# One packed word a record, and scatters without staging copies, in a graph network kernel

## The chip, the cores and the metric

The kernel runs on one NeuronCore of a Trainium2 chip. The metric is the time of one execution on the device in microseconds (us), median of several executions. The engines are TensorE (PE), VectorE (DVE), ScalarE (ACT), GpSimd (POOL) and SyncE (SP); 16 DMA engines move data between the on-chip memory (SBUF) and device memory. Indirect transfers, which take one row address a partition from a column of SBUF, are issued by POOL; plain ones by SP.

## The reference

6250 nodes with 128 features, 100000 edges with a source and a destination. Two GATv2 attention layers with three heads (self loops added), with batch norms and a skip path, and then one attention layer with eight heads, which sums over the edges of each source:

```python
edge_index = jnp.stack([src, dst])
h = jnp.maximum(_layernorm(x), 0.0)
x = x + _L0_gnn_ref(h, edge_index, ...)      # two GATv2 layers: softmax over the edges of each dst
h = jnp.maximum(_layernorm(x), 0.0)
x = x + _L1_gnn_ref(h, edge_index, ...)      # eight heads, summed over the edges of each src

# in a GATv2 layer
xl, xr = x @ Wl + bl, x @ Wr + br            # as (n, h, d)
e = leaky_relu(xl[src] + xr[dst], 0.2)
score = einsum('ehd,hd->eh', e, att)
ex = exp(score - segment_max(score, dst)[dst])
alpha = ex / segment_sum(ex, dst)[dst]
out = segment_sum(alpha[:, :, None] * xl[src], dst)
```

What is sorted is only the set of edges: the first two layers want the edges in order of blocks of 128 destinations, the last one in order of blocks of 128 sources.

## The kernel before

Before any attention the kernel sorts the edges by counting. An edge becomes a record of two 32-bit words, source and destination, in `pay` (125 partitions x 800 columns x 2). A record is put in its slot of a table in device memory, `rec_d` by destination and `rec_s` by source, by an indirect scatter: one scatter writes one column, 125 records. Slots that no edge takes keep a fill value, whose key is `PAD_KEY`.

The program is a chain of blocks. Inside a block each engine runs its own queue, in program order, and waits on semaphores; a block ends when all engines have ended it. The blocks that the change touches, in order:

- `constants`: VectorE makes the fill words (L234 to L237), SP writes them over both tables (L254) and waits for them.
- The key block of `sort_by_dst`: VectorE fills `pay` (L327, L328) and makes the one-hot inputs. A count block and a small block on the table of blocks follow.
- The rank block of `sort_by_dst`: for every group of 4 columns PE and VectorE find the slots (`pos_d`, written at L527, semaphore `ranked`). After all 800 columns VectorE scans for the sort by source (L678, L681, 49 times, once for each block of nodes). POOL scatters 49 columns of self loops (L539) and then `records.write(pool, 0, RANK_TURNS, ranked)`, 41 turns of 16 columns.
- `norm_to_features`: a layer norm on VectorE and ScalarE, with turns 41 to 44 of the scatters on POOL.
- `node_tables` of layer 1: the products with the layer's weights. PE multiplies a block of 128 nodes, ScalarE copies the result to one of two buffers (L1028), SP stores it (L991). POOL does turns 45 to 49. Layer 2 has the same block without scatters.
- `slot_tables`: SP loads the sorted records (L737) and the records at the row edges (L741, L742); VectorE splits them into the columns that the attention reads (L760 to L763 and on). It runs once for the order by destination and once for that by source.
- `gat_edges`, once a layer: 29 turns of 16 groups of 2 tiles of 128 slots. POOL gathers two tiles a group (L1121), and in 25 of the turns scatters one column of `rec_s` after each group (L1137), staged by L1131 and L1132 for 8 columns at a time. Each layer scatters half of the 800 columns.

A turn of the destination scatters is in a loop, so its columns have addresses that only a register knows. `scatter_columns` therefore copies 8 columns of records (L587) and 8 of slots (L588) to a fixed buffer, of which there are two, waits for both copies, and scatters from there (L592).

Of the kernel before, what the change touches and what calls it, by code (L numbers as in the profile page):

```python
# [12 lines left out]
ds = bass.ds  # L13
# [124 lines left out]
class Core:  # L138


    def __init__(self, nc, ctx):
# [23 lines left out]
        self.pay = sb("pay", [EC, COLS, 2], I32)  # L165
# [14 lines left out]
        self.rec_d = dram("rec_by_dst", [SLOTS, 2], I32)  # L180
        self.rec_s = dram("rec_by_src", [SLOTS, 2], I32)
# [33 lines left out]
def constants(k, io):  # L215
# [42 lines left out]
def sort_by_dst(k, io, beside):  # L258
# [20 lines left out]
    self_rec = cut(2 * NB, I32).rearrange("p (b f) -> p b f", f=2)  # L279
# [25 lines left out]
    with nc.Block() as block:  # L305
# [9 lines left out]
        def _(dve):  # L315
# [69 lines left out]
    with nc.Block() as block:  # L385
        @block.vector
        def _(dve):
# [9 lines left out]
            do(nc.vector.tensor_copy(self_rec[:, :, 0], k.node_i[:, :]))  # L397
            do(nc.vector.tensor_copy(self_rec[:, :, 1], k.node_i[:, :]))
# [20 lines left out]
    with nc.Block() as block:  # L419
# [116 lines left out]
        def _(pool):  # L536
            for b in range(NB):
                n = P if b < NB - 1 else TAIL
                pool.indirect_dma_start(k.rec_d, bass.IndirectOffsetOnAxis(ap=self_pos[0:n, b:b + 1], axis=0),  # L539
                                        self_rec[0:n, b, :], None).then_inc(scattered, 16)  # L540

            records.write(pool, 0, RANK_TURNS, ranked)
# [4 lines left out]
class Records:  # L547


    def __init__(self, k):  # L550
        self.k = k
        self.pos = k.gather_col[0:EC, 0:COLS]
        cut = Carver(k.lo_col)
        self.slot = [cut(CU, I32, EC) for _ in range(2)]
        self.rec = [cut(2 * CU, I32, EC).rearrange("p (u f) -> p u f", f=2) for _ in range(2)]
        self.written = [k.gather_sem(f"r_written{s}") for s in range(2)]
        self.staged = k.sem("r_staged")

    def write(self, pool, first, last, ranked=None):
        def turn(j):  # L560
# [1377 lines left out]
```

## Time and profile before

| | us |
|---|---|
| median of 3 runs | 7618.72 (7614.17 to 7625.17) |
| the profiled execution | 7605.49, its span 7603.6 |
| POOL busy | 5109.1, 67% of the span |
| VectorE busy | 5418.3, 71% |
| PE busy (matmul) | 4780.8, 63% |
| ScalarE busy | 3741.9, 49% |

The span is one execution from its first to its last instruction. POOL's busy time is nearly all indirect transfers, whose duration is that of making the descriptors and not of moving the data: 1856 gathers for the two layers (1906.2 us), 800 scatters by source (1135.5 us), 800 by destination (1032.2 us). In the 40 slices of the page, each 190 us long, VectorE and POOL are both busy in slices 2 to 7, and in slice 8 POOL works at 7 tenths beside 2 on VectorE and at most 4 elsewhere.

### The profile page before, as it was taken

What the parts mean: (1) busy time and instruction counts of PE and PEld (TensorE: products, weight loads), DVE (VectorE), ACT (ScalarE), POOL (GpSimd) and SP (SyncE); (2) the same over time, 40 slices, a digit from 0 to 9 for tenths busy, and PEclk for the clock granted to TensorE, in tenths of its full rate; (3) what the DMA queues carried; (4) which work ended last, traced back from release to release, by engine and by line L of the source; (5) the groups of instructions that cost most, each with busy time, mean ns of one, the idle gap of its engine ahead of it and who ended that gap; (6) DMA issues with size and microseconds to landing.
All of it is one profiled execution on the core that took longest, in us unless ns stands there. A gap on an engine that the chain in (4) does not pass through costs nothing. (4 is left out here: it accounts for less than half of the span.)

```text
span 7603.6 us, 122345 instructions
## 1 busy us (share of the span) xinstructions
PE 4780.8 (63%) x17049; PEld 2912.2 (38%) x17050; DVE 5418.3 (71%) x14343; ACT 3741.9 (49%) x17817; POOL 5109.1 (67%) x4746
## 2 busy tenths in 40 slices
PE   3555554045777777777876777777777855666663
PEld 2444441022333333333453333333333434555552
DVE  9766667226777777778955777777777964777776
ACT  4111114114777777777935777777777942000000
POOL 0677778766777777777505777777777602777773
PEclk9999999577999999999988999999999976777775
DMA  0556560123444444444604444444444602444443
GB/s 16 82 81 82 84 82 1 18 65 101 107 106 105 105 106 105 105 104 114 127 29 113 107 106 106 105 107 105 106 103 111 137 20 86 125 125 125 124 125 70
DMA packets 465689, 709.42 MB, mean 93 GB/s; under 512 B 171174, under 2 KB 340168, under 8 KB 464978
## 3 DMA queue, kind: packets, MB, share of 16 engines
q0 software_dynamic: 211488, 483.35, 26.3%
q1 hardware_dynamic: 254130, 225.33, 14.1%
q14 instruction: 52, 0.43, 0.0%
q8 instruction: 19, 0.31, 0.0%
HBM read 669.36 MB, written 35.78 MB: 93 GB/s over the span
## 5 line engine op out<-in xcount | busy, mean ns | idle before, releaser
L1121 POOL DMA_INDIRECT feat_area<-xl_table,feat_area x1856 | 1906.2, 1027 | 971.9 <-issue 514.9
L1211 PE MATMUL bank<-node_area,feat_area 128*128 x3712 | 1592.2, 555 | 1029.0 <-DVE feat_area L1346 909.5
L1301 ACT ACTIVATE feat_area<-feat_area 128x130 f32<-128x130 f32 x5568 | 1650.0, 298 | 1071.8 <-DVE feat_area L1354 1070.6
L1346 DVE TENSOR_TENSOR feat_area<-bank,feat_area 128x780 f32<-128x780 f32 x928 | 896.1, 966 | 845.0 <-DMA feat_area<-xl_table,feat_area 757.6
L1224 PE MATMUL bank<-feat_area 128*128 128x390 f32 x3712 | 1483.0, 524 | 20.2 <-DVE feat_area L853 6.6
L1285 ACT ACTIVATE feat_area<-feat_area 128x128 f32<-128x128 f32 x4640 | 1441.0, 386 | 0.8 <-DVE feat_area L1465 0.8
L1137 POOL DMA_INDIRECT rec_by_src<-feat_area x800 | 1135.5, 1419 | 304.6 <-issue 194.6
L1211 PEld LDWEIGHTS bank<-node_area,feat_area 128*128 128x128 f32 x3712 | 676.7, 202 | 1719.3 <-issue 1480.3
L592 POOL DMA_INDIRECT rec_by_dst<-lo_col x800 | 1032.2, 1290 | 301.1 <-issue 209.3
L1301 ACT ACTIVATION_READ_ACCUMULATOR feat_area<-feat_area 128x1 f32 x5568 | 1038.6, 187 | 0.0
L1714 POOL DMA_INDIRECT feat_area<-kv_table,feat_area x832 | 840.9, 1011 | 269.7 <-issue 252.5
L1224 PEld LDWEIGHTS bank<-feat_area 128*128 128x128 f32 x3712 | 744.7, 205 | 586.8 <-issue 165.5
L1354 DVE SCALAR_TENSOR_TENSOR feat_area<-feat_area 128x780 f32<-128x780 f32 x928 | 889.0, 958 | 0.0
L1752 PE MATMUL bank<-feat_area 128*128 128x136 f32 x1664 | 358.9, 379 | 436.8 <-DVE feat_area L1808 436.8
L443 ACT COPY node_area<-bank 128x49 f32<-128x49 f32 x800 | 160.5, 201 | 851.8 <-PE bank L461 758.5
L1764 ACT ACTIVATE feat_area<-feat_area 128x32 f32<-128x32 f32 x208 | 47.7, 229 | 1064.8 <-DVE feat_area L1796 1064.8
L853 DVE TENSOR_TENSOR feat_area<-iota_f,lo_col 128x256 f32<-128x256 f32 (+1 forms) x1136 | 525.3, 462 | 0.0
L1393 DVE SCALAR_TENSOR_TENSOR node_area<-node_area,stays,bank 128x390 f32 x812 | 494.6, 609 | 19.9 <-PE bank L1224 19.7
L1752 PEld LDWEIGHTS bank<-feat_area 128*128 128x128 f32 x1664 | 301.8, 263 | 486.1 <-DVE feat_area L1808 247.8
L463 PE MATMUL bank<-node_area 128*125 128x49 f32 x1600 | 473.9, 418 | 0.0
L461 PE MATMUL bank<-node_area 125*128 125x49 bf16 x800 | 176.3, 220 | 437.3 <-DVE node_area L517 433.4
L463 PEld LDWEIGHTS bank<-node_area 128*125 128x125 f32 x1600 | 411.9, 319 | 0.0
(269 smaller groups left out, 6188.1 us busy)
## 6 DMA issues: line engine op xcount, KB each, us to landing
feat_area<-lo_slot SPq DMA_DIRECT2D x672, 128.0 KB, 3.1
node_area<-in_dst SPq DMA_DIRECT2D x200, 250.0 KB
feat_area<-xl_table,feat_area POOLq DMA_INDIRECT x1856, 3.1
node_area<-lo_edge SPq DMA_DIRECT2D x200, 125.0 KB
xl_table<-feat_area SPq DMA_DIRECT2D x98, 195.0 KB, 2.3
feat_area<-kv_table,feat_area POOLq DMA_INDIRECT x832
rec_by_dst<-lo_col POOLq DMA_INDIRECT x800
rec_by_src<-feat_area POOLq DMA_INDIRECT x800, 2.7
```

The source lines that it names most:

```text
L463: nc.tensor.matmul(look[u], oh_loT[s][:, u * EC:(u + 1) * EC], table[u % 2], start=True, stop=True).then_inc(looked, 1)
L592: pool.indirect_dma_start(table, bass.IndirectOffsetOnAxis(ap=slot[:, u:u + 1], axis=0), rec[:, u, :], None).then_inc(written, 16)
L1121: pool.indirect_dma_start(ring[:, at:at + HE], None, k.xl, bass.IndirectOffsetOnAxis(ap=index[s // CG][:, n:n + 1], axis=0)).then_inc(gath ...
L1137: pool.indirect_dma_start(k.rec_s, bass.IndirectOffsetOnAxis(ap=slot[n][:, u:u + 1], axis=0), rec[n][:, u, :], None).then_inc(written[n], 16)
L1211: last = nc.tensor.matmul(pair[s % 2][:, u, 0:HE], pick[s // 2 % 2][:, c:c + P], k.node[:, ds(columns[0], HE)], start=True, stop=True)
L1224: last = nc.tensor.matmul(sums_in[s % 2], place[s % 2][:, u * P:(u + 1) * P], ring[:, at:at + HE], start=u == 0, stop=u == GS - 1)
L1285: last = nc.scalar.activation(row[:, 0:D], row[:, 0:D], ACT.Copy, scale=row[:, D:D + 1])
L1301: last = nc.scalar.activation(at, at, ACT.Copy, accum_out=score[s // CG][:, to:to + 1])
L1346: nc.vector.tensor_tensor(z[s % V].rearrange("p (u e) -> p u e", u=GS), pair[s % 2][:, :, 0:HE], ring[:, s * W:(s + 1) * W].rearrange("p ( ...
L1354: nc.vector.scalar_tensor_tensor(out=zu, in0=zu, scalar=0.0, in1=att_w.unsqueeze(1).to_broadcast([P, GS, HE]), op0=ALU.max, op1=ALU.mult). ...
L1714: pool.indirect_dma_start(kv[s][:, u * KV:(u + 1) * KV], None, k.kv, bass.IndirectOffsetOnAxis(ap=index[s][:, u:u + 1], axis=0)).then_inc( ...
L1752: nc.tensor.matmul(k.bank[2 + u][:, 0:VW], place[s % 2][:, u * P:(u + 1) * P], wv[s % 2][:, u * VW:(u + 1) * VW], start=True, stop=True).t ...
```

## The change

Node numbers fit 13 bits (`NODE_BITS`), so a record becomes one word: destination in the upper bits, source in the lower 13. `pay`, both tables, the fill values and the self-loop records have half the words. `PAD_KEY` becomes 8191, and `slot_tables` now takes a word apart with a mask and a shift, and marks padding with a compare, a product with 128 and an add, where before one mask kept the padding's bit.

The scatters of the sort by destination are written out one by one, with fixed addresses, straight from `pay` and the slots. The two copies and their wait go. Sixteen semaphores take the place of two: each scatter waits for the one 16 columns before it, and in the rank block every fourth also for its rank. The blocks' shares move: columns 0 to 683 are scattered in the rank block (656 before), 684 to 763 in the norm block (80, before 64), 764 to 799 in the table block (36, before 80).

```diff
-TURNS = COLS // CU // 2
-RANK_TURNS = TURNS * 41 // 50
-NORM_TURNS = TURNS * 45 // 50
-
-PAD_KEY = 16384
+DEEP = 16
+RANK_COLS = 684
+NORM_COLS = 764
+
+PAD_KEY = 8191
+NODE_BITS = 13
...
-        self.pay = sb("pay", [EC, COLS, 2], I32)
+        self.pay = sb("pay", [EC, COLS], I32)
...
-    fill_d, fill_s = cut(2 * SLOTROW, I32), cut(2 * SLOTROW, I32)
+    fill_d, fill_s = cut(SLOTROW, I32), cut(SLOTROW, I32)
...
-            do(nc.vector.memset(fill_d, 0))
-            do(nc.vector.memset(fill_s, 0))
-            nc.vector.memset(fill_d.rearrange("p (s f) -> p s f", f=2)[:, :, 1:2], PAD_KEY).then_inc(filled, 1)
-            nc.vector.memset(fill_s.rearrange("p (s f) -> p s f", f=2)[:, :, 0:1], PAD_KEY).then_inc(filled, 1)
+            nc.vector.memset(fill_d, PAD_KEY << NODE_BITS).then_inc(filled, 1)
+            nc.vector.memset(fill_s, PAD_KEY).then_inc(filled, 1)
...
-            do(nc.vector.tensor_copy(k.pay[:, :, 0], key["src"]))
-            do(nc.vector.tensor_copy(k.pay[:, :, 1], key["dst"]))
+            do(nc.vector.tensor_copy(part_i, key["src"]))
             do(nc.vector.tensor_copy(key_i, key["dst"]))
+            do(nc.vector.tensor_scalar(k.pay[:, :], key_i, NODE_BITS, None, ALU.logical_shift_left))
+            do(nc.vector.tensor_tensor(k.pay[:, :], k.pay[:, :], part_i, ALU.bitwise_or))
...
-            records.write(pool, 0, RANK_TURNS, ranked)
+            records.write(pool, 0, RANK_COLS, ranked)
...
-            for s in range(2):
-                if ranked is not None:
-                    pool.wait_ge(ranked, 4 * j + 2 * s + 2)
-                    pool.nop(nofuse=True)
-                scatter_columns(self.k, pool, self.pos, self.k.rec_d, self.rec[s], self.slot[s], self.staged,
-                                self.written[s], j, s)
...
+        k = self.k
+        for c in range(first, last):
+            n, turn = c % DEEP, c // DEEP
+            if ranked is not None and (c % 4 == 0 or c == first):
+                pool.wait_ge(ranked, c // 4 + 1)
+                pool.nop(nofuse=True)
+            if turn:
+                pool.wait_ge(self.written[n], 16 * turn)
+                pool.nop(nofuse=True)
+            pool.indirect_dma_start(k.rec_d, bass.IndirectOffsetOnAxis(ap=self.pos[:, c:c + 1], axis=0),
+                                    k.pay[:, c:c + 1], None).then_inc(self.written[n], 16)
...
-            do(nc.vector.tensor_copy(node_f, pair[:, :, gathered]))
-            do(nc.vector.tensor_scalar(lo_i, pair[:, :, key], PAD_KEY | (P - 1), None, ALU.bitwise_and))
+            do(nc.vector.tensor_scalar(near, raw, (1 << NODE_BITS) - 1, None, ALU.bitwise_and))
+            do(nc.vector.tensor_scalar(far, raw, NODE_BITS, None, ALU.logical_shift_right))
+            do(nc.vector.tensor_copy(node_f, part[gathered]))
+            do(nc.vector.tensor_scalar(lo_i, part[key], P - 1, None, ALU.bitwise_and))
+            do(nc.vector.tensor_scalar(part[1 - key], part[key], PAD_KEY, P, ALU.is_equal, ALU.mult))
+            do(nc.vector.tensor_tensor(lo_i, lo_i, part[1 - key], ALU.add))
...
-    rec = [cut(2 * CU, I32, EC).rearrange("p (u f) -> p u f", f=2) for _ in range(2)]
+    rec = [cut(CU, I32, EC) for _ in range(2)]
...
-                nc.gpsimd.tensor_copy(rec[n], k.pay[:, ds(c, CU), :]).then_inc(staged, 1)
+                nc.gpsimd.tensor_copy(rec[n], k.pay[:, ds(c, CU)]).then_inc(staged, 1)
```

POOL's queue in the rank block before, from the self-loop scatters to the first half turn of the loop; `lo_col` holds the two staging buffers:

```order
L539 DMA rec_by_dst<-node_area 131072x2 x49
L587 COPY lo_col<-pay 125x16 [waits r_ranked]
L588 COPY lo_col<-gather_col 125x8
L592 DMA rec_by_dst<-lo_col 131072x2 [waits r_staged]
L592 DMA rec_by_dst<-lo_col 131072x2 x7
...
L587 ISA [waits r_written0]
L587 COPY lo_col<-pay 125x16
L588 ISA
L588 COPY lo_col<-gather_col 125x8
L589 ISA
L592 DMA rec_by_dst<-lo_col 131072x2 [waits r_staged]
L592 DMA rec_by_dst<-lo_col 131072x2 x7
```

The same queue now, from the self loops over the first columns, and its end with the first columns of the norm block:

```order
L540 DMA rec_by_dst<-node_area 131072x1 x49
L566 DMA rec_by_dst<-pay,gather_col 131072x1 [waits r_ranked]
L566 DMA rec_by_dst<-pay,gather_col 131072x1 x3
...
L566 DMA rec_by_dst<-pay,gather_col 131072x1 [waits r_ranked,r_written0]
L566 DMA rec_by_dst<-pay,gather_col 131072x1 [waits r_written1]
...
L566 DMA rec_by_dst<-pay,gather_col 131072x1 [waits r_written11]
L420 UNCONDITIONAL_BRANCH [waits t_scat]
L882 UNCONDITIONAL_BRANCH [waits barrier_Pool_Activation_PE_DVE_SP_gather]
L566 DMA rec_by_dst<-pay,gather_col 131072x1 [waits r_written12]
```

The copies and their waits have left the queue, 684 scatters stand ahead of the block's end instead of 656, and nearly each has a wait of its own.

VectorE's queue in the block of `slot_tables` before, from the loaded records on:

```order
L760 CAST feat_area<-feat_area 128x1024
L761 TENSOR_SCALAR feat_area<-feat_area 128x1024
L762 CAST feat_area<-feat_area 128x1024
L763 CAST feat_area<-feat_area 128x1024
L764 CAST feat_area<-feat_area 1x1024
```

And now:

```order
L739 TENSOR_SCALAR feat_area<-feat_area 128x1024
L740 TENSOR_SCALAR feat_area<-feat_area 128x1024
L741 CAST feat_area<-feat_area 128x1024
L742 TENSOR_SCALAR feat_area<-feat_area 128x1024
L743 TENSOR_SCALAR feat_area<-feat_area 128x1024
L744 ISA feat_area<-feat_area 128x2048
L745 CAST feat_area<-feat_area 128x1024
L746 CAST feat_area<-feat_area 128x1024
L747 CAST feat_area<-feat_area 1x1024
```

Four instructions have come in ahead of the casts that release PE (L745) and SP (L746).

## Rows read from the trace of the kernel before

**Rows 1.** Lines of POOL, 281.7 to 1146.5 us: count | busy us, mean ns | idle.
```profile
L592 POOL DMA_INDIRECT rec_by_dst<-lo_col x520 | 639.7, 1230 | 195.6 <-issue 134.7 <-POOL lo_col L588 57.0 <-DMA rec_by_dst<-lo_col 2.7
```

**Rows 2.** Timeline of POOL, quiet stretch: start us, us, instruction, idle before.
```profile
1339.35 0.21 POOL L587 COPY lo_col<-pay 125x16 int32 x1
...
1340.55 1.20 POOL L592 DMA_INDIRECT rec_by_dst<-lo_col  x1 [0.87 <-POOL lo_col L588]
1342.05 1.17 POOL L592 DMA_INDIRECT rec_by_dst<-lo_col  x1 [0.30 <-issue]
```

**Rows 3.** Timeline of VectorE, from the scans to the end of the norm.
```profile
1162.58 1.88 DVE L678 TENSOR_TENSOR_SCAN feat_area<-feat_area 125x800 f32<-125x800 f32 x1
1164.49 0.99 DVE L681 TENSOR_TENSOR feat_area<-feat_area 125x800 f32<-125x800 f32 x1
...
1293.93 1.18 DVE L685 CAST pos_s<-bank 125x400 int32<-125x400 f32 x2 [1.77 <-PE bank L697]
1432.32 0.17 DVE L937 MEMSET feat_area<- 128x128 f32 x1 [137.21 <-PEq L419]
...
1509.40 0.29 DVE L944 COPY feat_area<-bank 128x128 f32<-128x128 f32 x1 [0.42 <-PE bank L929]
```

**Rows 4.** Timeline of POOL, starts of norm and table block, and two long instructions.
```profile
1432.56 0.20 POOL L587 COPY lo_col<-pay 125x16 int32 x1 [3.76 <-POOLq L419]
...
1456.93 7.46 POOL L592 DMA_INDIRECT rec_by_dst<-lo_col  x1 [0.30 <-issue]
...
1477.16 6.13 POOL L587 COPY lo_col<-pay 125x16 int32 x1
...
1551.62 0.20 POOL L587 COPY lo_col<-pay 125x16 int32 x1 [4.64 <-POOLq L896]
```

**Rows 5.** Lines of POOL, 1146.5 to 1293 us.
```profile
L592 POOL DMA_INDIRECT rec_by_dst<-lo_col x52 | 116.8, 2245 | 19.8 <-issue 13.7 <-POOL lo_col L588 6.1
```

**Rows 6.** Timeline of SP: the stores of the table blocks, layer 1 and 2.
```profile
1568.36 125.11 SPq L991 DMA_DIRECT2D xl_table<-feat_area  x49
...
3962.61 70.69 SPq L991 DMA_DIRECT2D xl_table<-feat_area  x49
```

**Rows 7.** Transfers: KB each, median us to landing; 1568 to 1681, 3962 to 4033.
```profile
xl_table<-feat_area SPq DMA_DIRECT2D x41, 195.0 KB, 4.9
...
xl_table<-feat_area SPq DMA_DIRECT2D x49, 195.0 KB, 2.2
```

**Rows 8.** Waits of POOL, 1800 to 3400 us: total, times, longest.
```profile
POOL feat_area L1121 <- issue: 192.5, 632, 0.3
```

**Rows 9.** Timeline of VectorE in the constants and key blocks.
```profile
1.26 1.76 DVE L234 MEMSET node_area<- 128x2048 int32 x1 [1.12 <-PEq L1928]
...
6.64 0.91 DVE L237 MEMSET node_area<- 128x1024 int32 x1 [0.16 <-issue]
...
26.56 0.58 DVE L327 CAST pay<-node_area 125x800 int32<-125x800 f32 x1
```

**Rows 10.** Waits of SP, 0 to 217 us.
```profile
SPq L223 <- DMA rec_by_src<-node_area: 5.5, 1, 5.5
```

**Rows 11.** Lines of ScalarE, 1567 to 1605 us.
```profile
L1028 ACT COPY feat_area<-bank 128x390 f32<-128x390 f32 x13 | 6.3, 484 | 43.8 <-DMA xl_table<-feat_area 26.4 <-PE bank L1012 17.4
```

**Rows 12.** Timeline of VectorE in `slot_tables`.
```profile
1702.47 0.69 DVE L760 CAST feat_area<-feat_area 128x1024 f32<-128x1024 int32 x1 [6.53 <-DMA feat_area<-rec_by_dst]
...
1711.56 1.22 DVE L781 TENSOR_TENSOR feat_area<-feat_area 128x1023 f32<-128x1023 f32 x1
```

**Rows 13.** Line 1131: ns min/median/max, first and last start us.
```profile
L1131 POOL COPY feat_area<-pay x100: 201/501/949, 1745.9 to 5828.6; 125x16 int32 x96, 125x16 int32<-125x16 int32 x4
```

**Rows 14.** The page, costliest groups: busy us, mean ns | idle before.
```profile
L1121 POOL DMA_INDIRECT feat_area<-xl_table,feat_area x1856 | 1906.2, 1027 | 971.9 <-issue 514.9
```

**Rows 15.** Line 539: ns min/median/max.
```profile
L539 POOL DMA_INDIRECT rec_by_dst<-node_area x49: 954/958/1625, 217.6 to 280.1; - x49
```

**Rows 16.** Line 587, its register instructions.
```profile
L587 POOLq FUSED_REGOPS  x98: 64/69/81, 300.1 to 1660.0; - x98
```

More of the change, by code:

```diff
@@ L178, in dram @@
             return nc.dram_tensor(name, shape, dt, kind="Internal").ap()
-        self.rec_d = dram("rec_by_dst", [SLOTS, 2], I32)
-        self.rec_s = dram("rec_by_src", [SLOTS, 2], I32)
+        self.rec_d = dram("rec_by_dst", [SLOTS, 1], I32)
+        self.rec_s = dram("rec_by_src", [SLOTS, 1], I32)
         self.lo_edge = dram("lo_edge", [E], BF16)
@@ L552, in __init__ @@
         self.pos = k.gather_col[0:EC, 0:COLS]
[L553 to L557, printed above, removed]
-    def write(self, pool, first, last, ranked=None):
-        def turn(j):
-            for s in range(2):
-                if ranked is not None:
-                    pool.wait_ge(ranked, 4 * j + 2 * s + 2)
-                    pool.nop(nofuse=True)
-                scatter_columns(self.k, pool, self.pos, self.k.rec_d, self.rec[s], self.slot[s], self.staged,
-                                self.written[s], j, s)
-        if first == 0:
-            turn(0)
-        with pool.Fori(max(first, 1), last) as i:
-            turn(i)
-        if last == TURNS:
-            for s in range(2):
-                pool.wait_ge(self.written[s], 16 * CU * TURNS)
@@ L577, in scatter_columns @@
-def scatter_columns(k, pool, pos, table, rec, slot, staged, written, j, s, n=CU, first=0):
-    nc = k.nc
-    step = 2 * j + s
-    if reused(j):
-        pool.wait_ge(written, 16 * n * j)
-        pool.nop(nofuse=True)
-    nc.gpsimd.tensor_copy(rec, k.pay[:, ds(step * n + first, n), :]).then_inc(staged, 1)
-    nc.gpsimd.tensor_copy(slot, pos[:, ds(step * n + first, n)]).then_inc(staged, 1)
-    pool.wait_ge(staged, 2 * step + 2)
-    pool.nop(nofuse=True)
-    for u in range(n):
-        pool.indirect_dma_start(table, bass.IndirectOffsetOnAxis(ap=slot[:, u:u + 1], axis=0),
-                                rec[:, u, :], None).then_inc(written, 16)
+        self.written = [k.gather_sem(f"r_written{s}") for s in range(DEEP)]
@@ new lines, in write @@
+    def write(self, pool, first, last, ranked=None):
+        k = self.k
[9 more added lines that the diff above has]
+                                    k.pay[:, c:c + 1], None).then_inc(self.written[n], 16)
+        if last == COLS:
+            for n in range(DEEP):
+                pool.wait_ge(self.written[n], 16 * (COLS // DEEP))
@@ L711, in slot_tables @@
     cut = Carver(k.wide)
-    raw = cut(2 * SLOTROW, I32)
-    pair = raw.rearrange("p (s f) -> p s f", f=2)
+    raw = cut(SLOTROW, I32)
+    near, far = cut(SLOTROW, I32), cut(SLOTROW, I32)
+    part = {0: near, 1: far}
     node_f = cut(SLOTROW)
@@ L740, in _ @@
                 sp.wait_ge(edges_set, 1)
-                sp.dma_start(edge_i[1:P, 0:2], rec_rows[0:P - 1, SLOTROW - 1, :]).then_inc(loaded, 16)
-                sp.dma_start(edge_i[0:P - 1, 2:4], rec_rows[1:P, 0, :]).then_inc(loaded, 16)
+                with nc.allow_non_contiguous_dma(reason="one word per partition"):
+                    sp.dma_start(edge_i[1:P, 0:1], rec_rows[0:P - 1, SLOTROW - 1, :]).then_inc(loaded, 16)
+                    sp.dma_start(edge_i[0:P - 1, 1:2], rec_rows[1:P, 0, :]).then_inc(loaded, 16)
             sp.wait_ge(lo_ready, 1)
@@ L776, in _ @@
                 do(nc.vector.tensor_scalar(k.into_col[:, :], at, float(SPARE), None, ALU.add))
-                do(nc.vector.tensor_copy(key_f, pair[:, :, key]))
+                do(nc.vector.tensor_copy(key_f, part[key]))
+                do(nc.vector.tensor_scalar(edge_i, edge_i, NODE_BITS, None, ALU.logical_shift_right))
                 do(nc.vector.tensor_copy(edge_f, edge_i))
@@ L899, in _ @@
             def _(pool):
-                records.write(pool, RANK_TURNS, NORM_TURNS)
+                records.write(pool, RANK_COLS, NORM_COLS)
         if load is not None:
@@ L999, in _ @@
             def _(pool):
-                records.write(pool, NORM_TURNS, TURNS)
+                records.write(pool, NORM_COLS, COLS)
         @block.tensor
```

17 lines of the change are left out of this document (9 added, 8 removed).

## The prediction

> **What bounds the kernel now.** I read the page first: in the 40 slices GpSimd (POOL) works from the first scatters until the attention of layer 1 ends, and in slices 7 and 8 nearly nothing else does. So I took POOL's rows by stage and asked at each stage's end which engine was last.
>
> Sort and rank stage, 217 to 1431 us. POOL scatters 49 columns of self loops and then 656 of the 800 edge columns. From 281.7 to 1146.5 us it gets 520 of them out, 864.8/520 = 1.663 us a column [rows 1]. A scatter is 1.18 us in a quiet stretch, with 0.30 us between two; every eighth follows two staging copies, and there the gap from scatter to scatter is 1.19 us [rows 2], 0.89 more. VectorE's last work of the stage is at 1293.9, its next at 1432.3 behind a 137 us idle [rows 3]: POOL alone ends this stage, at 1428.8 (1432.56 less its 3.76 idle) [rows 4].
>
> While VectorE scans, a scatter takes 2.245 us in the mean [rows 5], and starts follow each other in 2.945 us, one iteration of scan and product: 1.88 and 0.99 us with what lies between [rows 3]. 49 such iterations end at 1292.2, so they begin at 1147.8. 49 iterations, 49 columns: the staging copies sit inside waits there and cost nothing.
>
> Norm stage, to 1551 us: VectorE has finished at 1509.7 [rows 3], POOL works to 1547.0 (1551.62 less 4.64) [rows 4]. POOL ends this stage too, with 64 columns in 1547.0 - 1432.6 = 114.4 us, of which 12.2 are one scatter and one copy held by two 6.7 us vector operations [rows 4].
>
> Table stage of layer 1, to 1696 us: the last 80 columns. Its 49 stores take 125.1 us, the same 49 stores of layer 2, with no scatter beside them, 70.7 us [rows 6]. A store lands in 4.9 us beside scatters and in 2.2 without [rows 7]. POOL finishes at 1680 and ends nothing here, but its scatters slow the stores, and each pair of output buffers waits for them.
>
> Attention of both layers: POOL waits only for its own issue, 0.3 us each time [rows 8], so it paces 25 of the 29 turns of each layer.
>
> **The change part by part.**
>
> *Constants.* Four memsets, the first at 1.26 us and the last ending at 7.55 [rows 9], become two of 0.91 us that need no order: about 3.1 us. 4.4 saved. The two fills are 1 MB each and the stage waits 5.5 us for them [rows 10]; half the bytes I take at 2.1 less (0 to 2.75). Sum -6.5 us, bounds -4.4 to -7.2.
>
> *Keys.* Two casts of 0.58 us into pay [rows 9] become a cast, a shift and an or of two inputs. The or is at 0.99 us, as the product of the same 125x800 shape [rows 3]: +1.0 us. All of it is ahead of the counting, so on the path.
>
> *Rank stage.* A column now costs 1.230 + 0.302 = 1.532 us in the first stretch (mean of [rows 1] with the gap of [rows 2]). By 1147.8 POOL has done 866.1/1.532 = 565 columns, where it had done 521. 49 more go with the scans, 614 at 1292.2. The change asks for 684 here instead of 656: 70 are left, 103.7 us at 1.482, to 1395.9. Against 1428.8 that is -33 us. VectorE stays covered: it ends 102 us earlier. All 800 columns are ranked before the scans begin, 930 us after the stage's start, 1.16 a column, and POOL starts on them 64 us late, so `ranked` holds nobody.
>
> Each column now has a wait of its own for the scatter 16 before it, and every fourth one for `ranked`. Behind the waiting instruction stands the whole of POOL, and behind POOL the stage. A scatter 16 back is 23 us old, and landing is a matter of a few us ([rows 7] for stores). What the instruction itself costs no scatter shows, but the gathers of attention do: every second has one or two waits and a nop ahead, and 632 of them sit idle 192.5 us, 0.305 each, longest 0.3 [rows 8]. That is the gap without any wait [rows 2]. I take 0. Bounds: 0, and 0.57 us a column, which is the 0.87 gap behind the wait on POOL's own copies less 0.30 [rows 2]; nearest is the gather, whose semaphores are other engines' and queues', as here.
>
> The Trainium skill says, under Runtime: NRT & Kernel Launch, Instruction fetch mechanics, that code is fetched in blocks ahead of execution and crossing one is mostly hidden, while taken branches break the prefetch. By it the written-out code costs nothing and a loop the more. No row of POOL here shows straight code as long as 684 columns.
>
> *Norm stage.* 80 columns instead of 64: 80 x 1.482 + 12.2 = 130.8 us against 114.4, +16.4 us. POOL still ends it, 53 us behind VectorE, so this is paid in full. The two 6.7 us operations will hold POOL as before.
>
> The Trainium skill has this hold as a rule (SBUF — State Buffer, SBUF: two separate sides): GpSimd can't write descriptors while VectorE has the shared port pair. The trace agrees: 7.46 us for a scatter that otherwise takes 1.18. By that rule shorter scatters would win nothing beside the scans; a sum that gave the scan stretch 144/1.482 = 97 columns would come out 71 us faster.
>
> *Table stage.* 36 columns instead of 80, over at 1551.6 + 36 x 1.482 = 1605. Up to 1605 ScalarE had handed over 13 blocks [rows 11]; the other 36 go at layer 2's pace, 70.7/48 = 1.47 us: 53 us, last store at 1658 instead of 1693.5. -35 us. Bounds: nothing, if the stores are slow for another reason than the scatters; and -39, at 1.47 us for all but the blocks before the last scatter with a tighter start.
>
> *Slot tables, twice.* Added on VectorE: two extractions and a compare at 0.69 us (the cast of 128x1024, [rows 12]) and an add of two inputs at 1.22 [rows 12]: 3.3 us, twice, and 0.2 for the edges. The integer add is a form that no row shows: 0.7 to 4 us. The load of 512 KB instead of 1 MB saves about 1 us each. The edge loads stay 127 rows of one record and land last in layer 1. Sum +5 us, 0 to +9.
>
> *Staging of the sort by source.* 100 copies of 125x16 words, median 0.501 us [rows 13], lose half their words; the shortest is 0.201, so most of the median is a wait for the port and not words. I take 0.04 us off each: -4 us, 0 to -7, paid out in full because POOL paces both layers.
>
> *Bytes.* 4 instead of 8 a record leave the number of rows per scatter as it is. 128 rows of 1560 bytes are gathered in 1.027 us [rows 14], 128 self records of 8 bytes scattered in 0.958 [rows 15], so POOL's time doesn't follow bytes: 0.
>
> Sum: -6.5 + 1.0 - 33 + 16.4 - 35 + 5 - 4 = -56 us. The profiled execution took 7605.5 (span 7603.6 and 1.9 around it), so 7549 by its own time. It is 13.2 below the median of the runs; the forecast for the median is 7618.7 - 56 = 7562 us.
>
> **Rivals.**
>
> A, slower: each written-out column pays for its wait and its nop. A register instruction of POOL's sequencer takes 0.069 us [rows 16]; two of them a column, 764 columns on the path, are +107 us: 7669. It decides from 56/764 = 0.073 us a column; from 0.093 it is slower than can be told from none. Against it stand the gathers [rows 8]; for it, that those waits come once in three instructions and here with every one.
>
> B: the stores of the table stage are not freed (or are as slow beside fewer, denser scatters as long as it matters). Then -21 remains: 7598. Against it the landing of 4.9 and 2.2 us [rows 7].
>
> C: scatters become shorter. The self-loop scatters of 128 rows take 0.958 us, those of 125 rows 1.18 [rows 2]. If not the rows but the staged source is the cause, 764 x 0.22 = 170 us more go: 7392. Against it: the longest self scatter, 1.625 us [rows 15], is the last, which has 106 rows, so it is the count that isn't 128 that costs.
>
> D, the change does nothing that counts: POOL's gain is given back by the 28 and 16 columns moved forward. By the sum these cost 41 + 24 us of the 49 + 7 gained, and without the table stage that is nearly so: it is B.
>
> **How the numbers follow.** Forecast 0.66, its own range 7535 to 7585 by the bounds above. A 0.10, B 0.18, C 0.03, something not listed (mostly within 0.2% of before) 0.03. A change under 0.2%, 15 us, can't be told from none here. Faster: forecast, nearly all of B (7598 is 21 below, with an error of 8 two thirds of it and more), C: 0.66 + 0.13 + 0.03 = 0.82. Same: 0.05 of B, 0.02 of A at a small price, 0.03 other: 0.10. Slower 0.08. The range 7528 to 7606 takes in B and leaves out A and C.
>
> **What would show it.** POOL: gap of 0.30 ahead of all 800 scatters, 1.18 us each; 0.37 or more ahead of them is A, 0.96 a scatter is C. Rank stage: POOL ends about 1390 on the new axis (1395.9 less the 5.5 of the head), VectorE's idle about 100 us. Norm stage about 131 us of POOL. Table stage: stores over some 90 us instead of 125, landing of 2.2 us in its second half; 120 or more is B. Attention: no change of turn. The forecast is wrong if the gap ahead of scatters grows, or if the stores don't speed up when POOL is done.

## The result, and the profile after

The changed kernel takes 7985.28 us (median, 7982.22 to 8004.11) against 7618.81 for the kernel before on the same chip: ratio 1.0486, 95% interval 1.0467 to 1.0504. It is 4.9% slower, where I forecast 7562 us. The profiled span is 7980.5 us against 7603.6, 376.9 more.

The rows of the page that changed most, slices of 199.5 us first, then two costliest groups and the queues of the DMA engines:

```profile
DVE  9533343592577777777895677777777974777776
POOL 0775565407377777777740777777777620777773
DMA  0687788712344444444451444444444531444443
...
q0 software_dynamic: 211488, 482.52, 24.8%
q1 hardware_dynamic: 254130, 223.23, 20.2%
...
L566 POOL DMA_INDIRECT rec_by_dst<-pay,gather_col x800 | 967.2, 1209 | 741.9 <-issue 463.5
...
L495 DVE TENSOR_SCALAR node_area<-node_area,part_f 128x500 f32<-128x500 bf16 x200 | 103.5, 518 | 806.3 <-DMA node_area<-lo_edge 802.9
```

The rank stage now reaches to the end of slice 9 (1793.8 us; before to 1432.6, in slice 8), and from slice 2 to 8 the DMA engines stand at 6 to 8 tenths. In the kernel before they stood at 5 to 6, from slice 2 to 6. VectorE waits 803 us for the loads of `lo_edge` in its rank loop; POOL, which was to be freed, stands idle. SP's timeline has the borders of the stages (start, length):

```profile
1793.81 0.86 SPq L844 DMA_DIRECT2D feat_area<-in_x  x1
...
1931.05 0.62 SPq L964 DMA_DIRECT2D feat_area<-in_L_gnn_Wl  x1
...
1950.26 103.49 SPq L975 DMA_DIRECT2D xl_table<-feat_area  x49
2056.06 0.33 SPq L715 DMA_DIRECT2D feat_area<-rec_by_dst  x1
```

Where the 377 us went, in us, each border against the same one of before (1432.58, 1551.30, 1695.81 us; attention starts at 1743.65 before and 2105.82 after). The slot tables here are those of layer 1; the second ones are in the last row.

| stage | before | after | difference | forecast |
|---|---|---|---|---|
| to the start of the norm | 1432.6 | 1793.8 | +361.2 | -38.5 |
| norm | 118.7 | 137.2 | +18.5 | +16.4 |
| table stage of layer 1 | 144.5 | 125.0 | -19.5 | -35 |
| slot tables | 47.8 | 49.8 | +1.9 | about +2 |
| attention and all behind it | 5860.0 | 5874.7 | +14.7 | about -1 |

So one stage holds nearly everything. Its end is VectorE's now. Timeline of VectorE in the changed kernel:

```profile
1791.77 1.18 DVE L662 CAST pos_s<-bank 125x400 int32<-125x400 f32 x2 [1.77 <-PE bank L674]
1793.54 0.17 DVE L921 MEMSET feat_area<- 128x128 f32 x1 [0.59 <-PEq L420]
```

And of POOL, which ended this stage in [rows 3, 4] while VectorE stood idle (the cut is marked):

```profile
1538.33 1.18 POOL L566 DMA_INDIRECT rec_by_dst<-pay,gather_col  x1 [3.84 <-DVE gather_col L528]
1539.82 1.17 POOL L566 DMA_INDIRECT rec_by_dst<-pay,gather_col  x1 [0.30 <-issue]
...
1794.28 1.18 POOL L566 DMA_INDIRECT rec_by_dst<-pay,gather_col  x1 [250.29 <-issue]
```

POOL's scatters are as fast as forecast, 1.18 us behind a gap of 0.30, but most fourth ones wait for a rank, and POOL has been idle 250 us when VectorE is done. The lookups of the rank loop, one ScalarE copy of line 443 (444 after) a column, run from 217.5 to 1141.6 us before and from 212.2 to 1639.4 after; the scans behind them take the same 150 us.

Queues and issues from 600 to 800 us, a stretch inside the loop (packets, MB, share of 16 engines), in the kernel before:

```profile
q1 hardware_dynamic: 12142, 16.18, 52.0%
q0 software_dynamic: 3842, 0.26, 3.8%
...
node_area<-in_dst SPq DMA_DIRECT2D x42, 250.0 KB
...
rec_by_dst<-lo_col POOLq DMA_INDIRECT x120
```

In the changed kernel:

```profile
q1 hardware_dynamic: 6938, 9.25, 69.5%
q0 software_dynamic: 3089, 0.16, 5.0%
...
node_area<-in_dst SPq DMA_DIRECT2D x25, 250.0 KB
...
rec_by_dst<-pay,gather_col POOLq DMA_INDIRECT x99
```

VectorE's wait for the loads in the same stretch (us, times, longest), before and after:

```profile
DVE node_area L494 <- DMA node_area<-lo_edge: 69.6, 28, 5.4
```

```profile
DVE node_area L495 <- DMA node_area<-lo_edge: 118.0, 23, 10.2
```

A share times 16 engines times 200 us, over the packets, is the time of one packet: of the loads (q1) 137 ns before, 320 after. Each packet of a load, as large as before, holds its engine 2.3 times as long, beside fewer scatters. The loop takes a pair of loads per four columns: 42 in 200 us before, 25 after. The scatters' own packets take 32 ns before and 52 after here, but 33 after from 700 to 900 us, so they don't tell the two kernels apart.

The stores of the table stage point the same way. Beside scatters, 1950 to 1983 us, seven stores land in 9.7 us at the median ([rows 7] had 4.9):

```profile
xl_table<-feat_area SPq DMA_DIRECT2D x7, 195.0 KB, 9.7
```

From 1986 to 2053 us, without scatters:

```profile
xl_table<-feat_area SPq DMA_DIRECT2D x41, 195.0 KB, 2.2
```

The input is sorted by destination (the reference sorts it when it makes the inputs) and a column is 125 consecutive edges, so its records go to nearly consecutive slots. With two words they fill 1000 bytes of DRAM 8 bytes apart, with one word 500 bytes, 4 apart. The theories:

1. Neighbouring writes: what slows the loads is that the scattered writes lie closer (1a) or are smaller (1b).
2. Way of issue: the payload read in place, the written-out code, or sixteen semaphores.
3. Placement: the smaller table moved the tensors behind it in DRAM.

### The profile page after: what moved, and what is told of

Same layout as the page of the kernel before. It is cut to its first block and busy times, and to the rows that moved or that the text cites. A ratio compares the mean times of both kernels' runs of the same rounds, so it can differ in the third digit from the quotient of the medians.

```text
span 7980.5 us, 122310 instructions
## 1 busy us (share of the span) xinstructions
PE 4768.7 (60%) x17049; PEld 2908.7 (36%) x17050; DVE 5422.1 (68%) x14351; ACT 3741.9 (47%) x17817; POOL 4994.6 (63%) x4546
## 3 DMA queue, kind: packets, MB, share of 16 engines
q1 hardware_dynamic: 254130, 223.23, 20.2%
## 5 line engine op out<-in xcount | busy, mean ns | idle before, releaser
L566 POOL DMA_INDIRECT rec_by_dst<-pay,gather_col x800 | 967.2, 1209 | 741.9 <-issue 463.5
L495 DVE TENSOR_SCALAR node_area<-node_area,part_f 128x500 f32<-128x500 bf16 x200 | 103.5, 518 | 806.3 <-DMA node_area<-lo_edge 802.9
## 6 DMA issues: line engine op xcount, KB each, us to landing
node_area<-lo_edge SPq DMA_DIRECT2D x200, 125.0 KB
```

## The experiments

A ratio below is that to the kernel before on the same chip. Chips differed: the kernel before took 8104 us on one of them and 7607 to 7640 on the others, so times are compared only where the chip is the same. Borders and packet times come from one trace of each kernel; where they stand beside those of another chip, the text says so. "This stretch" is 600 to 800 us.

**Two words, written out.** The kernel before with the new way of issue alone:

```
-            rec = lo_col copy, slot = lo_col copy, 41 of 50 turns
+            pool.indirect_dma_start(k.rec_d, ...ap=self.pos[:, c:c + 1]..., k.pay[:, c, :], None)
+RANK_COLS = 684; NORM_COLS = 764; DEEP = 16
```

> The written-out scatters of the changed kernel, straight from the payload and with sixteen semaphores, but each record still two words (8 bytes) in a table of two-word slots. Theory 1 (small writes): a column's 125 records go to neighbouring slots, and what slows the loads of the rank loop is that these slots are now 4 bytes apart, all in about 500 bytes of DRAM. Then this kernel's loads of in_dst and lo_edge are as before: about 140 ns a packet on q1 in the rank loop (before 137, after 296) and 4.6 to 4.8 us a group of four columns (after 7.8); the norm stage begins near 1395 us instead of 1794, and the time is 7550 to 7620. Theory 2 (way of issue): reading the payload without a copy, the written-out code or the sixteen semaphores slow the loads. Then it stays near 7.8 us a group, q1 near 290 ns a packet, and the time is 7950 to 8010.

Measured: 7614.59 us, 0.9976 of before (0.9957 to 0.9996). Theory 2 falls as the cause of the 377 us: the way of issue makes no slow kernel. But the loop is slower than expected, with 37 pairs of loads (5.4 us each) and 165 ns a packet in this stretch, and the norm stage begins at 1423.5 us instead of near 1395. VectorE ended the rank stage here, and POOL had been idle:

```profile
1424.00 1.18 POOL L565 DMA_INDIRECT rec_by_dst<-pay,gather_col  x1 [30.84 <-issue]
```

About 5 us of that idle time stand at such a border even where POOL comes last, so some 26 us of POOL's gain were lost.

**One word, staged.** The changed kernel with the old loop:

```
-RANK_COLS = 684; NORM_COLS = 764
+        nc.gpsimd.tensor_copy(rec, k.pay[:, ds(step * n + first, n)])   # and slot, then 8 scatters
```

> The changed kernel's one-word records, but written with the staging copies, the loop and the two semaphores of the kernel before, and with its shares. Theory 1 (small writes): the loads of the rank loop are slow as in the changed kernel, q1 at 270 to 310 ns a packet, the norm stage begins at 1750 to 1850 us, and the time is 7940 to 8080. Theory 2 (way of issue): q1 near 140 ns a packet, the norm stage near 1430 us, the time 7600 to 7640.

Measured: 8104.43 us, 1.0609 (1.0575 to 1.0643), norm stage from 1853.8. From 600 to 800 us:

```profile
q1 hardware_dynamic: 6121, 8.20, 86.1%
...
rec_by_dst<-lo_col POOLq DMA_INDIRECT x104
```

450 ns a packet, more than the 270 to 310 expected, and the time is over the expected 7940 to 8080. One word is slow however it is issued.

**One word, 8 bytes apart.** The table has two words a slot and only the first is written; ranks are doubled where they are added up:

```
-        self.rec_d = dram("rec_by_dst", [SLOTS, 1], I32)
+        self.rec_d = dram("rec_by_dst", [PITCH * SLOTS, 1], I32)       # PITCH = 2
-                nc.vector.tensor_tensor(pos_d[...], before[s], peers[s], ALU.add)
+                nc.vector.scalar_tensor_tensor(out=pos_d[...], in0=before[s], scalar=float(PITCH), in1=peers[s], ...)
```

> The changed kernel with one-word records at a pitch of two words: each write is still 4 bytes, but slots are 8 bytes apart as before. If what counts is how closely the writes lie (theory 1a), q1 is near 140 ns a packet in the rank loop and the time 7550 to 7620. If the size of the write counts (theory 1b, 4 bytes against 8), it stays near 296 ns and 7985 plus at most 10 for the longer fill and load of the table. The table is 0.5 MB larger, which moves what is allocated behind it; the next kernel tells that apart (theory 3).

Measured: 7630.39 us, 0.9985 (0.9971 to 0.9998), norm stage from 1406.5:

```profile
q1 hardware_dynamic: 10938, 14.60, 59.3%
...
rec_by_dst<-pay,gather_col POOLq DMA_INDIRECT x130
```

173 ns a packet with 4-byte writes: not the 140 expected, but what 8-byte writes took on this chip (165). The size of a write is not it (1b falls); its distance to the next one is, unless it is the placement.

**The table moved.** Twice the allocation, first half used, slots 4 bytes apart:

```
-        self.rec_d = dram("rec_by_dst", [SLOTS, 1], I32)
+        self.rec_d = dram("rec_by_dst", [2 * SLOTS, 1], I32)           # rec_d[0:SLOTS] filled and read
```

> The changed kernel with the table of records by destination allocated twice as long and only its first half used, so that all later DRAM tensors lie as in the kernel with pitch 2, while slots stay 4 bytes apart. Theory 1: as the changed kernel, 296 ns a packet and 7980 to 8000 us. Theory 3 (lo_edge and the table came to lie in unlucky places of the DRAM): near 140 ns and 7550 to 7620.

Measured: 8105.6 us, 1.061 (1.0589 to 1.0631), 386 ns a packet. Theory 3 falls: this kernel and the one at 8 bytes allocate alike and ran on one chip, and they differ only in the distance between slots and the fill and load that go with it (1.061 against 0.9985). The 120 us over the changed kernel asked for that kernel once more, unchanged:

> The changed kernel once more, on the chip of the runs beside it: the kernel with the moved table took 8106 us and its rank stage ended at 1884 us, 90 later than the changed kernel had it. If placement alone makes that difference, this run is near 7985 with a norm stage that begins near 1794; if chips differ in how dear the neighbouring writes are, it is anywhere between 7980 and 8110, with q1 near 330 ns a packet in the rank loop as in the moved one.

Measured: 8574.47 us on a chip where the kernel before takes 8104.39: 1.0575 (1.0534 to 1.0616), 352 ns a packet. The time is outside the expected 7980 to 8110, which supposed an ordinary chip. In ratio it agrees with the moved table; the first chip's 1.0486 was the mildest. On that slow chip the kernel before gave a trace too:

> The kernel before on the same chip, for its trace: all theories expect q1 near 137 ns a packet in the rank loop, a norm stage that begins at 1425 to 1435 us, and 7620 to 7645 us.

Measured: 8104.17 us, norm stage from 1480.5, 175 ns a packet. My 7620 to 7645 was of another chip. The changed kernel doubles the packet there as well (175 to 352). Here VectorE ended the rank stage even in the kernel before, with POOL idle for 62.7 us ahead of the norm stage, so a POOL with less to do can win nothing in that stage. Of the 498 us by which this trace is longer than the first chip's, 447 lie behind the start of attention (6306.7 us against 5860.0); why the chip is slower stays open.

**One word, 16 bytes apart** (PITCH = 4), on the slow chip:

> The changed kernel with one-word records at a pitch of four words (16 bytes). If the loads suffer in proportion to how many records share a stretch of DRAM (slope), the loads gain once more over pitch 2: q1 at 110 to 125 ns a packet in the rank loop against 143, the norm stage begins at 1370 to 1395 us instead of 1406, and the time is 7575 to 7620. If it is a cliff between 4 and 8 bytes (two records in one 8-byte word), q1 stays at 135 to 150 ns, the norm stage at 1400 to 1412, and the time within 15 us of the kernel with pitch 2, the longer load of the table included.

Measured: 8090.09 us, 0.9986 (0.9958 to 1.0014): no difference that can be told. 147 ns a packet, between what the two theories expected, but the norm stage begins at 1520.5, later than the 1480.5 of before; VectorE ends the rank stage again. Its waits in this stretch show another bound (waited for, us, times, longest):

```profile
DVE node_area L520 <- PE bank L466: 57.0, 43, 2.7
DVE node_area L497 <- DMA node_area<-lo_edge: 13.3, 9, 3.2
DVE node_area L520 <- remote: 11.7, 11, 1.3
```

**Other shares**, 704 and 776 columns at 8 bytes apart, same chip:

> One-word records at a pitch of two words, with 704 columns in the rank stage instead of 684 and 776 by the end of the norm stage instead of 764. The pitch-2 kernel's scatters stood idle for some 35 us at the end of the rank stage while VectorE scanned, so 20 more columns at 1.48 us fit there; 24 are left for the table stage instead of 36. The norm stage should take 107 to 122 us of scatters instead of 118 to 134, the table stage up to 18 us less beside scatters: 10 to 25 us faster than the pitch-2 kernel, 0.995 to 0.997 of the kernel before. Were the loads of the rank loop slowed further by the added columns, the norm stage would begin after 1415 us and nothing would be won.

Measured: 8145.26 us, 1.005 (1.0024 to 1.0076), norm stage from 1540.9. The expectation failed: VectorE ended the rank stage, with POOL idle for 170 us in spite of its 20 columns more. The 8-byte kernel with the old shares did not run on this chip, so whether shares or chip cost the time stays open.

**Two words, written out, again; and staged until the end of the rank stage.** The second keeps the rank stage of before:

```
+            records.write_staged(pool, RANK_TURNS, ranked)     # rank stage, 656 columns, as before
+                records.write(pool, RANK_COLS, NORM_COLS)      # 656 to 736, written out
+                records.write(pool, NORM_COLS, COLS)           # 736 to 800, written out
```

> The written-out scatters of two-word records once more, on the chip of the two runs beside it: 0.995 to 1.000 of the kernel before (0.9976 measured), q1 at 155 to 185 ns a packet in the rank loop, norm stage from 1410 to 1530 us as the chip goes, table stage's stores 85 to 97 us.

> The kernel before with its staged two-word scatters in the rank stage (41 of 50 turns, 656 columns), and the written-out ones only behind it: 80 columns in the norm stage, 64 in the table stage. If the closer pace of the written-out scatters is what slows VectorE's rank loop (37 groups of four in 200 us against 42), the rank stage is as in the kernel before and the gain behind it is whole: norm 118 us of scatters where 64 staged columns took 114, stores 100 to 108 us instead of 125: 15 to 27 us faster than the kernel before, 0.9965 to 0.998. If the pace does not matter and the difference of 42 and 37 groups was one of chips, this is as fast as the kernel before less the same 15 to 27 us, and the two-word kernel written out throughout beats it, since its rank stage would be shorter by up to 33 us on the same chip.

Measured on one chip: 7583.21 us, 0.9941 (0.9924 to 0.9957), a little better than expected, and 7632.61, 1.0004 (0.9994 to 1.0013), which has none of the 15 to 27 us expected by either branch. Norm stage from 1413.4 and 1444.4: the written-out scatters are worth 31 us in the rank stage. Both kernels issue 38 pairs of loads in this stretch (153 and 167 ns a packet), but one stretch does not tell the whole loop. Its lookups, written out and staged:

```profile
L443 ACT COPY node_area<-bank x800: 200/202/204, 217.9 to 1224.8; 128x49 f32<-128x49 f32 x160
```

```profile
L445 ACT COPY node_area<-bank x800: 200/202/203, 218.1 to 1187.1; 128x49 f32<-128x49 f32 x160
```

The loop ends 38 us later beside written-out scatters. With one word at 4 bytes it is the same: 1518.1 us of loop written out (the moved table), 1487.6 staged, on one chip. These are one trace each, and whether the closer pace or another part of the way of issue does it is not shown. On this chip it does no harm, because POOL still comes last. Timeline of POOL in the first of the two:

```profile
1407.09 1.18 POOL L565 DMA_INDIRECT rec_by_dst<-pay,gather_col  x1 [0.30 <-issue]
1413.83 1.18 POOL L565 DMA_INDIRECT rec_by_dst<-pay,gather_col  x1 [5.57 <-issue]
```

VectorE at the same border:

```profile
1377.39 1.19 DVE L661 CAST pos_s<-bank 125x400 int32<-125x400 f32 x2 [1.77 <-PE bank L673]
1413.10 0.17 DVE L913 MEMSET feat_area<- 128x128 f32 x1 [34.52 <-PEq L419]
```

POOL ends the stage, as in [rows 3, 4], but VectorE's idle time is down to 34.5 us (103.1 in the second kernel). On the chip of the first two-word run the same kernel had none left. The second kernel's norm stage takes 133.8 us from border to border and its table stage 132.6; on the first chip the kernel before took 118.7 and 144.5. So what the table stage won was about what the 16 more columns in the norm stage cost.

**Fewer scatters under way.** The changed kernel with DEEP = 2:

> The changed kernel (one word, 4 bytes apart) with two semaphores instead of sixteen, so that no more than two scatters are under way at a time. If neighbouring writes hurt because many scatters in flight hold the same stretch of DRAM, q1 falls from 296 to 350 ns a packet to under 220, and the time falls by more than 100 us, unless the waits for landings (2.7 to 4.9 us each with two in flight) slow POOL below two columns in 4 us. If the writes within one scatter are enough, q1 stays at 280 ns a packet or more, and the time is at or above that of the changed kernel (1.05 to 1.07 of the kernel before).

Measured: 9789.93 us, 1.2832 (1.2807 to 1.2858). The packet falls to 224 ns, close to the under 220 of the first theory, and the exception that the theory named came true: POOL waits for landings. Behind the rank loop, where no other transfer runs, it issues 408 scatters in 1600 us, two at a time. Queues from 1600 to 1800 us:

```profile
q0 software_dynamic: 1600, 0.08, 2.9%
...
rec_by_dst<-pay,gather_col POOLq DMA_INDIRECT x51
```

So with the DMA engines 2.9% busy a scatter still takes 3.92 us, or 7.84 from issue to landing with two under way. What it waits for does not show as busy time of the engines. The next four measure one scatter by itself, with DEEP = 1.

> The changed kernel with one semaphore: each scatter waits until the one before it has landed, so the distance between scatters behind the rank loop, where no load runs, is the landing of one of them. With two under way they came 3.92 us apart (408 in 1600 us), so 7.84 us each from issue to landing. If the conflict is within one scatter (its 125 words of 4 bytes lie next to each other), the distance is 6 to 8 us here and the time 9900 to 13000 us. If it is between scatters that overlap, one alone lands in 2.5 to 4 us, the distance is 3 to 4.5 us, and the time is at most about that of the run with two (9790).

> The same with the words 8 bytes apart. If neighbouring 4-byte writes cost time in a scatter of their own, this one's distance behind the rank loop is 2.5 to 4.5 us, at least 1.5 times shorter than at 4 bytes. If the writes of one scatter do not disturb each other at 4 bytes either, both distances are equal.

> The same with the words 16 bytes apart. Slope: 0.85 of the distance at 8 bytes or less (q1's packets went from 180 to 147 ns in the rank loop of the runs with sixteen under way). Cliff between 4 and 8 bytes alone: within 5% of it.

> Two-word records (8 bytes, 8 bytes apart), written out, one scatter at a time. If only the distance of the writes counts, it is as one word at 8 bytes (within 5%); if full 8-byte words are cheaper than halves of them, it is shorter by 0.3 us or more.

Times 12452, 10272, 9264 and 10212 us (kernel before 7607), one execution each. Quiet stretches: start and end, length, POOL's busy time on scatters and their count (the other columns are clock, DMA share and GB/s). At 4 bytes:

```profile
1600.00:3600.00 2000.00, 305.41 (x259) 0.50 0.02 0
```

At 8 bytes:

```profile
1600.00:3600.00 2000.00, 494.05 (x419) 0.50 0.02 0
```

At 16 bytes, half as long a stretch:

```profile
1500.00:2500.00 1000.00, 339.62 (x289) 0.50 0.03 1
```

With two words, 8 bytes apart:

```profile
1600.00:3600.00 2000.00, 496.42 (x422) 0.50 0.03 0
```

Their landing over all 800, from the lines of the scatter (at 4 bytes the trace pairs none). At 8 bytes:

```profile
DMA to landing us min/median/max: 3.3/3.9/9.6
```

At 16 bytes:

```profile
DMA to landing us min/median/max: 2.5/2.6/8.7
```

With two words:

```profile
DMA to landing us min/median/max: 3.2/3.9/9.3
```

From one scatter to the next: 7.72, 4.77, 3.46 and 4.74 us (4.77 is over the 2.5 to 4.5 expected; the other expectations held). Landing is 0.86 less where the trace has both, so 3.9, 2.6 and 3.9, and at 4 bytes an estimated 6.9. Three readings. The conflict is inside one scatter, which is slow with nothing beside it; and with two under way each takes about as long (7.84) as one alone (7.72). It is a slope: doubling the distance takes 3.0 us off, then 1.3. And one word costs what two do at the same distance. How far the slope goes on, the scatters by source can tell, whose slots lie all over their table. The pages of the kernel before, with 8-byte records, and of the changed one, with 4-byte ones, have the same line:

```profile
rec_by_src<-feat_area POOLq DMA_INDIRECT x800, 2.7
```

2.7 us, beside the gathers of attention, is about what 16 bytes apart take, for 4-byte and 8-byte writes alike. So more distance than that need not win anything. The scatters' packets take 58 to 62 ns in all four kernels (q0's share from 1600 to 2400 us), so the cost does not show there. The rank loop issues 22, 32 and 41 of them in 200 us here, and still VectorE waits 73.6, 49.5 and 31.2 us for `lo_edge`: a third to a half fewer scatters, more harm. The two-word kernel, with 32, waits 48.0.

These runs don't take apart the distance between neighbours and the length of DRAM that one scatter covers (500, 1000, 2000 bytes), and all of them write in rising order. No kernel with the same slots in another order was run.

**8 and 16 bytes side by side**, sixteen under way:

> One-word records 16 bytes apart, sixteen scatters under way, as before, on one chip with the kernel at 8 bytes. A scatter alone lands in 2.6 us here against 3.9 at 8 bytes and about 6.9 at 4. If that slope still reaches the rank loop, its loads no longer set VectorE's pace (13 us of waits for lo_edge in 200 us, where the others had 60 to 84), the norm stage begins 5 to 30 us earlier than at 8 bytes, the longer load of the table takes 3 to 6 us of it back, and the time is 0.990 to 0.996 of the kernel before. If the lookup chain between PE, ACT and VectorE takes the bound over (57 us of VectorE's waits in 200 us on the other chip), the time is that of 8 bytes plus the 3 to 6 us.

> One-word records 8 bytes apart on the same chip. It was 0.9985 of the kernel before on one chip, where two-word records written out were 0.9976, and those were 0.9941 on another: 0.993 to 0.999 here, norm stage from 1400 to 1420 us.

Measured: 7586.66 us, 0.997 (0.9958 to 0.9981) at 16 bytes, 7597.86, 0.9982 (0.9973 to 0.9991) at 8. The first misses its 0.990 to 0.996, the second is as expected. The lookups of the rank loop (min/median/max ns, first and last start), at 16 bytes:

```profile
L446 ACT COPY node_area<-bank x800: 200/200/202, 218.7 to 1002.8; 128x49 f32<-128x49 f32 x160
```

At 8 bytes:

```profile
L446 ACT COPY node_area<-bank x800: 199/199/200, 214.7 to 1155.9; 128x49 f32<-128x49 f32 x160
```

The wider distance ends the loop 153 us earlier, with 50 pairs of loads in this stretch against 41. None of it reaches the stage's end: the norm starts at 1406.4 and 1403.3, because POOL with 684 columns at 1.48 us ends it (VectorE is idle for 249.5 and 93.4 us). The stores gain 7.5 us (83.2 against 90.7), the load of the larger table takes 2.3 longer to issue (6.05 against 3.80). The mechanism expected for no gain, the lookup chain, is not what took the bound over on this chip.

The best versions are the written-out two-word kernel (0.9976 and 0.9941) and the one-word kernel at 16 bytes (0.997); they were not run side by side. None wins more than 0.6%.

## Why the prediction was wrong

The step that failed is *Bytes*: "POOL's time doesn't follow bytes: 0". For POOL it held (1.178 us at the median). But with tables packed tight, bytes also decide how close the records lie in DRAM, and the sum had no term for what that does to other transfers. With it fell the line under *Rank stage*, "VectorE stays covered: it ends 102 us earlier". VectorE ended the stage, 250 us after POOL had run out of work. Its cover rested on a rank loop that depends on loads, and the trace of before had that in VectorE's wait for `lo_edge`, 69.6 us from 600 to 800 us; I read it as slack, not as the place where a slower load comes through. Point by point:

- *Constants* and *keys*: the head of the kernel is 5.3 us shorter (first lookup at 212.2 against 217.5); forecast -5.5. Right.
- *Rank stage*, -33: +366.5 (the +361 of the table, and the 5 that the head gave). The loop grew by 503 us (924 become 1427); the first 137 of them vanished in the idle time that VectorE had at the end of the stage. With two-word records 8 bytes apart the term is right on one chip: -31 (1413.4 against 1444.4), and POOL ends the stage. So the arithmetic on POOL stood. The cover did not hold everywhere even so: on another chip VectorE ended the stage of that same kernel, at 1423.5, and beside written-out scatters the loop is 38 us longer than beside staged ones. That part does not come from the 4-byte distance, and the prediction had no term for it either.
- `ranked` "holds nobody": false in the changed kernel (258.5 us of POOL's idle time), true at 8 bytes (6.4 us).
- *Waits and nops at 0* (rival A at +107): right. The gap stays 0.30 us ahead of scatters that wait for nothing.
- *Norm stage*, +16.4: +18.5. Right.
- *Table stage*, -35: -19.5. Mis-sized, and it fits the same cause: landing beside the 4-byte scatters is 9.7 us and not 4.9. With two words written out it is 5.0, the stores take 91.1 us, and the stage 111.5 against 144.5 before (another chip): -33.
- *Slot tables*, +5 for both: +1.9 in layer 1, and from the load of the records by source to the first gather behind it 23.7 us instead of 20.2, +3.5. Right. The integer add, whose bounds of 0.7 to 4 us had no row, takes 1.23 us.
- *Staging*, -4: not there. The median copy takes 0.494 us instead of 0.501.
- *Attention*: its rhythm is unchanged, landings of 3.1 and 2.7 us in both. Of the +14.7 us of the last row 3.5 are the second slot tables; most of the rest, 11.2 us, lies between the first store of layer 2's table stage and the records by source, and is not explained. With sixteen scatters under way, or the staging of before, the spans behind the start of attention are 5860 to 5887 us for two-word kernels and 5875 to 5907 for one-word ones on the ordinary chips, one trace of each, where the runs of one kernel lie up to 60 us apart. So whether one word costs anything there can't be told. Records by source go to slots all over their table, so few there are close together.
- Rivals: A and C are refuted by the gap and the 1.18 us, B (stores not freed) holds by half. None of the three was what happened. A rival "the loads of the rank loop get slower" was needed, and its place was visible. D sets the 41 and 24 us of the moved columns against "the 49 + 7 gained"; by the terms of the sum (-33 and +16.4 are what is left) it is 74 + 7.

The Trainium skill, under DMA: Bandwidth & Descriptors, Specifications, says that a transfer under 512 B is a read-modify-write. That would let every write here, 4 or 8 bytes, be dear, and fits that both cost the same at one distance. It would make no difference between before and after. No run shows whether the writes here are made so. What the runs add is the distance: 6.9 (estimated), 3.9, 2.6 us a scatter. That such rewrites of one stretch of DRAM wait for each other is my reading of it; no run here looks inside the DRAM.

## What to carry to other kernels

Before making scattered records smaller, ask where they land: if one scatter writes neighbouring slots, packing them closer can cost landing time and slow the loads and stores beside it, as here, and a few bytes of padding can be cheaper than the bytes saved. When an engine is "covered", look at what it waits for in its own loop; 137 us of cover were gone here when its loads' packets took 2.3 times as long. Price a change on each queue that shares DRAM with it, not on the issuing engine alone.

## What the runs showed that I had not expected

- One indirect scatter of 125 words lands in some 6.9 (estimated), 3.9 and 2.6 us with the words 4, 8 and 16 bytes apart, with nothing beside it and DMA engines 1.5 to 3.4% busy. It shows in the landing and in the packets of others (137 to 320 ns), not in the scatters' own.
- One scatter at 4 bytes every 9 us (22 in 200) makes VectorE wait 73.6 us for its loads. 32 two-word ones, also one at a time and on the same chip, make it wait 48.0, and the 120 of the staged two-word kernels 69.6 to 80.3 on three chips.
- Beside written-out scatters the rank loop is 38 us longer than beside staged ones on the same chip (1006.9 and 969.0 us).
- A chip can cost as much as the change did: the kernel before took 8104 us on one and 7607 to 7640 on the others. Packets of the loads don't tell such a chip: it had 175 ns, an ordinary one 167 beside the same staged scatters, and the first 137.
